# 128 rows of zeros behind both tables of edge sums, in a graph kernel on one core

## What is computed

```
dst = jnp.minimum((50000 * jax.random.uniform(..., (50000,)) ** 2.0).astype(jnp.int32), 49999)
_o = jnp.argsort(dst, stable=True)

# layer 0, added to x: attention over the incoming edges, gate, feed-forward
a = jnp.exp(alpha - m[dst])
denom = jax.ops.segment_sum(a, dst, num_segments=n) + 1e-16
a = a / denom[dst]
out = jax.ops.segment_sum(a[:, :, None] * v_j, dst, num_segments=n)
...
h2 = jax.nn.relu(h2 @ W1.T + b1) @ W2.T + b2

# layer 1, added to x: normalised sum over the incoming edges
x_i = x[from_]
x_j = x[to_]
m_j = norm[:, None] * (x_j + x_j * x_i @ W1_w.T + W1_b)
out = jax.ops.segment_sum(m_j, to_, num_segments=n)
```

## Time and profile before

| | us |
|---|---|
| timed executions: lowest, median, highest | 3546.07, 3553.65, 3562.57 |
| the profiled execution | 3554.38 |
| its span (first to last instruction) | 3552.5 |
| phase C, from the first fetch to the last | 3011.0 to 3533.4 |

### The profile page before, as it was taken

One profiled execution on the slowest core, in us unless ns is written; L12 is line 12 of the kernel. 1 busy time (PEld: TensorE's weight loads), 2 busy tenths in 40 slices (PEclk: granted clock), 3 DMA queues, 4 the chain that ended last, 5 costly groups with the idle time before them and its releaser, 6 DMA issues. The chain is left out here.

```text
span 3552.5 us, 56630 instructions
## 1 busy us (share of the span) xinstructions
PE 2248.5 (63%) x13730; PEld 1803.6 (51%) x13730; DVE 2280.3 (64%) x9173; ACT 1722.7 (48%) x4075; POOL 2301.1 (65%) x2429
## 2 busy tenths in 40 slices
PE   0002777777777773799999999997443442455554
PEld 0002667766667762566666666665333332444444
DVE  8886666666666664677877787775111111678778
ACT  8994333333333331678887888886111111344343
POOL 5554777777777771555555555551777775777776
PEclk9998999999999995899999999999555555555555
DMA  6553233333333332233333333341566664456676
GB/s 204 177 176 94 82 101 92 91 101 91 91 101 91 91 101 62 65 105 107 107 100 102 108 104 102 101 109 67 124 129 130 132 131 113 118 149 152 144 147 133
DMA packets 253888, 401.93 MB, mean 113 GB/s; under 512 B 56515, under 2 KB 165456, under 8 KB 253728
## 3 DMA queue, kind: packets, MB, share of 16 engines
q1 hardware_dynamic: 183670, 265.77, 25.2%
q0 software_dynamic: 63424, 133.57, 18.6%
q10 hardware_dynamic: 6682, 1.46, 0.2%
HBM read 241.74 MB, written 160.29 MB: 113 GB/s over the span
## 5 line engine op out<-in xcount | busy, mean ns | idle before, releaser
L1159 POOL DMA_INDIRECT agg<-rows,at_n x392 | 388.8, 992 | 144.4 <-issue 111.1
L1651 POOL DMA_INDIRECT aggc<-rows,at_nc x392 | 398.8, 1017 | 113.2 <-issue 104.8
L628 POOL DMA_INDIRECT zs<-z_table,at_s x392 | 381.0, 972 | 112.9 <-issue 104.7
L628 POOL DMA_INDIRECT zd<-z_table,at_d x392 | 375.0, 957 | 119.4 <-issue 105.7
L1476 POOL DMA_INDIRECT h2s<-h_table,at_s x392 | 372.8, 951 | 113.2 <-issue 90.9
L1224 PE MATMUL p_f<-z_t,w_t 128*128 128x512 f32 x784 | 377.4, 612 | 64.1 <-ACT act L1294 64.0
L1529 PE MATMUL p_sum<-h2s,same 128*128 128x129 f32 x784 | 208.1, 438 | 307.8 <-DMA h2s<-h_table,at_s 244.4
L1235 PE MATMUL p_f<-w_t,act 128*128 128x128 f32 x3136 | 383.8, 278 | 0.0
L1235 PEld LDWEIGHTS p_f<-w_t,act 128*128 128x128 f32 x3136 | 361.2, 192 | 22.2 <-issue 22.2
L1529 PEld LDWEIGHTS p_sum<-h2s,same 128*128 128x128 f32 x784 | 173.3, 318 | 342.5 <-issue 264.8
L1516 DVE TENSOR_SCALAR same<-dst_sb,dst_g 128x128 f32<-128x128 uint16 x392 | 84.0, 303 | 400.8 <-DMA dst_sb<-dst 392.5
(11 more groups left out here) (317 smaller groups left out, 6471.9 us busy)
## 6 DMA issues: line engine op xcount, KB each, us to landing
rows<-rows_sb SPq DMA_DIRECT2D x49, 576.0 KB
h_table<-h2b SPq DMA_DIRECT2D x49, 516.0 KB, 2.9
rows<-rows_sb SPq DMA_DIRECT2D x49, 516.0 KB
xa<-in_x_dram SPq DMA_DIRECT2D x49, 512.0 KB, 3.8
z_table<-za SPq DMA_DIRECT2D x49, 512.0 KB, 2.9
dst_sb<-dst SPq DMA_DIRECT2D x98, 256.0 KB
xb<-in_x_dram SPq DMA_DIRECT2D x49, 512.0 KB, 4.0
x_table<-x1b SPq DMA_DIRECT2D x49, 512.0 KB, 4.7
```

What stands on the lines that cost most here:

```text
L628: pool.indirect_dma_start(out=to[:, slot, k], out_offset=None, in_=z_table, in_offset=bass.IndirectOffsetOnAxis(ap=at[:, slot, k:k + 1], a ...
L1159: pool.indirect_dma_start(out=agg[:, ring, k], out_offset=None, in_=rows0, in_offset=bass.IndirectOffsetOnAxis(ap=at_n[:, ring, k:k + 1], ...
L1651: pool.indirect_dma_start(out=agg[:, slot, k], out_offset=None, in_=rows1, in_offset=bass.IndirectOffsetOnAxis(ap=at_n[:, slot, k:k + 1], ...
```

## The change

Behind the rows of the edges, both tables get 128 rows of zeros instead of one. The zeros in SBUF from which they are written grow from one partition to 128. POOL makes a column `none_at` with EP + p in partition p, by one more IOTA and one more copy. The middle takes this column in place of the number EP, so that a node without an edge fetches row EP + (its number modulo 128). The loops of B and C are untouched, and so is the zero row of `z_table`.

```
-    rows0 = dram("rows0", [EP + 1, ROW0])
-    rows1 = dram("rows1", [EP + 1, ROW1])
+    rows0 = dram("rows0", [EP + P, ROW0])
+    rows1 = dram("rows1", [EP + P, ROW1])
...
+        none_at = sb("none_at", [P, 1])
...
-            zrow = t("zrow", [1, ROW0])
+            zrow = t("zrow", [P, ROW0])
+            none_i = t("none_i", [P, 1], I32)
...
-                    act.dma_start(rows0[EP:EP + 1, :], zrow[:]).then_inc(padded, 16)
-                    act.dma_start(rows1[EP:EP + 1, :], zrow[:, 0:ROW1]).then_inc(padded, 16)
+                    act.dma_start(rows0[EP:EP + P, :], zrow[:]).then_inc(padded, 16)
+                    act.dma_start(rows1[EP:EP + P, :], zrow[:, 0:ROW1]).then_inc(padded, 16)
...
+                    chain.mark(g.iota(none_i[:], pattern=[[1, 1]], base=EP, channel_multiplier=1))
...
+                    g.tensor_copy(none_at[:], none_i[:]).then_inc(consts_set, 1)
...
-                    dve.wait_ge(consts_set, 2)
+                    dve.wait_ge(consts_set, 3)
...
-                    chain.mark(v.tensor_scalar(none[:], deg[:], 0.5, float(EP), ALU.is_lt, ALU.mult))
+                    chain.mark(v.tensor_scalar(none[:], deg[:], 0.5, none_at[:], ALU.is_lt, ALU.mult))
```

More of the change, by code:

```diff
@@ L408, in _ @@
                     act.dma_start(src_pad[E:EP].rearrange("(a b) -> a b", a=16), pad_z[:, 0:n].bitcast(I32)).then_inc(padded, 16)
-                    act.dma_start(z_table[N:N + 1, :], zrow[:, 0:D]).then_inc(padded, 16)
-                    act.dma_start(rows0[EP:EP + 1, :], zrow[:]).then_inc(padded, 16)
-                    act.dma_start(rows1[EP:EP + 1, :], zrow[:, 0:ROW1]).then_inc(padded, 16)
+                    act.dma_start(z_table[N:N + 1, :], zrow[0:1, 0:D]).then_inc(padded, 16)
+                    act.dma_start(rows0[EP:EP + P, :], zrow[:]).then_inc(padded, 16)
+                    act.dma_start(rows1[EP:EP + P, :], zrow[:, 0:ROW1]).then_inc(padded, 16)
                     nodes_a_scalar(act)
```

## The result

The changed kernel takes 3572.64 us (median of 7 executions, 3565.9 to 3575.66), the kernel before 3556.51 (7, 3546.07 to 3562.57). The ratio is 1.0043, with a 95% interval of 1.0029 to 1.0058: slower by about 15 us by the ratio, 16 by the medians. The forecast was 3569. The profiled execution took 3573.41 us, 3571.7 of them its span, against 3552.5 before: 19.2 us more. In the changed kernel the lines of B and C stand four higher (`aggc` L1655, `mixed` L1724, the two `basec` L1725 and L1727, `x1c` L1630, `leaky` L1736).

The account below looks back on a forecast made before the run. PE covers phase B's fetches and POOL paces phase C's; 26 groups by +0.79 and 13 by -0.38 us give +15.6, so 3554.4 + 15.6 = 3570.0, less 0.7 for the timed runs: 3569 us, range 3538 to 3584.

Parts of the forecast that it names:

- The zero rows and the column: At the start: larger zero writes, one IOTA, one CAST and the column operand cost 0, at most about 1 us once.
- Fetches in B land sooner: Phase B: fetches land up to 0.5 us sooner each, but PE covers them, so 0.
- Landings of C fall below the edge: Phase C: groups then alternate between late and early landings, +0.79 us each, +30.8 us if it holds through groups 9 to 47.
- L: Phase C: delay from the end of a group's last POOL call to DVE's `mixed`; expected 1.6 to 1.85 us.
- the edge: Phase C: delay between 1.61 and 1.87 us, last call to `mixed`; just above it a group hardly stalls, below it stalls.
- The price of the alternation: Phase C, groups 9 to 47: 26 alternating by +0.79 us and 13 at their best by -0.38, together +15.6 us.
- the alternation: Phase C: late and early landings in turn, SP's `x1c` load ahead of POOL's last call; 11.37 us a group.
- Just above the edge: Faster rival, phase C: landings settle where groups hardly stall, -14.8 us, 3540, or 3531 without the early spell; chance 0.20.
- Landings don't move: Rival: something other than the shared address slows late fetches, or the change is hidden; 3554 us, 3547 to 3562; chance 0.25.
- Nearly throughout: Slower rival, phase C: late and early landings alternate in 29 or more of 39 groups, up to 3585 us; chance 0.27.
- The rule of the Trainium skill on reads that start off a 256 byte boundary: Fetches: such reads take extra beats or transactions, so zero rows would get dearer and no landing sooner; spoke against the change.
- the saw: Phase C: POOL's stall against the delay from last call to `mixed`, repeating every 1.25 us, the distance of two calls.

Follow-up runs that it names:

- e1: Changed kernel, but all nodes without an edge fetch one address, the first of the 128 zero rows: 3554.77 us, 0.9993 of the kernel before.
- e2: Changed kernel with spread zero rows in phase B only, one address in phase C: 3554.84 us, 0.9994 of the kernel before.
- e4: Changed kernel with two small pause steps on DVE ahead of `mixed` in phase C: 3539.23 us, 0.995 of the kernel before.
- e9: Changed kernel using eight zero rows, one per fetch: 4124.87 us, 1.0041, on another chip where the kernel before took 4111.64 us.
- e10: Changed kernel using 16 zero rows, each 8 apart, the same in every fetch: 4124.35 us, 1.0029, on a chip where the kernel before took 4111.64 us.
- e11: Changed kernel, first `basec` of phase C made from one SBUF input, without bias: 4096.55 us, 0.998, on a chip where the kernel before took 4111.64 us.
- e8: Changed kernel with SP's load of `x1c` in phase C held until POOL has made the group's last call: 3548.52 us, 0.9957 of the kernel before.
- e6: Changed kernel with twelve pause steps on DVE ahead of `mixed` in phase C: 3544.3 us, 0.9951 of the kernel before.
- e5: Changed kernel with six pause steps on DVE ahead of `mixed` in phase C: 3564.65 us, 1.001 of the kernel before.

## Why the prediction was right, step by step

- **The zero rows and the column: 0.** Confirmed by e1 (0.9993).
- **Fetches in B land sooner, worth 0.** Confirmed: 2.5 us in place of 3.1, B of the same length with the same two waits, and e2 (0.9994). The forecast had said 2.6 to 2.8.
- **Landings of C fall below the edge.** Confirmed. L of the prompt groups is 1.62 to 1.84, and the edge lies between 1.71 and 1.83, as the copy goes; the prediction had it between 1.61 and 1.87 and took 1.6 to 1.85 for L. So the landings straddle the edge, and a good stretch never lasts.
- **The price of the alternation.** Here two terms were off, against each other. The prediction took two thirds of the groups 9 to 47 as alternating at 11.37 us and one third at their best, 26 by +0.79 and 13 by -0.38, +15.6. Measured: 34 of 39 are outside the good stretches, at (429.64 - 50.89)/34 = 11.14 each, where 50.89 is what groups 26 to 28 and 41 to 42 take together. So 34 by +0.56 and 5 by -0.40 came out, +17.0. The extent was too small and the price too high. That the forecast lay within 4 us of the time is luck in this part: the measured extent at the price taken would have been 34 by 0.79 less 5 by 0.38, +25, and the extent taken at the measured price 26 by 0.56 less 13 by 0.40, +9. The alternation is cheaper than in groups 2 to 8 because a late landing there is often only 3.6 to 4.1 us behind. DVE has then caught up by the next group (L = 1.77 in the rows above), and the calls behind it cost 1.0 us more than in a group at its best (11.10 us for group 14); after one of 4.5 us it has not (L = 2.61), and they cost 1.9 more (12.02 for group 4). A pair takes 21.8 us in the first case (groups 14 and 15) and 22.5 in the second (groups 4 and 5).
- **Not in the sum:** the last group, +2.0, which ended in the bad state, and 1.05 ahead of group 2. The latter is also just over the 1 us that the prediction allowed the phases before C; by the starts of C in e1 and e2 (3011.61 and 3008.53, with the same phases ahead of it) it is within what varies from one to another.
- **The rivals.** "Just above the edge" fell, though e4 shows that its price was right: with L at 1.85 to 2.1 in most groups the kernel takes 3539, where the rival said 3540. "Landings don't move" fell: they move, and by e1, e9 and e10 the shared address is the cause. "Nearly throughout" (3573 and more) was close: by extent it is what happened, by time it is the forecast's upper end.
- **The rule of the Trainium skill on reads that start off a 256 byte boundary** (DMA: Bandwidth & Descriptors, How a descriptor splits into AXI transactions), by which no landing would come sooner, did not decide. Of the changed kernel's rows of zeros for B, 576 bytes apart, three in four start off such a boundary if the table starts on one (that it does is assumed), and a packet takes 0.153 us against 0.218 with the single aligned row. In e10 all 16 are aligned, at 0.147, against 0.153 in e11 on the same chip, where three in four are not; for these rows the rule is worth no more than this difference.

**What holds POOL.** The prediction knew the saw, not its law. Laid side by side, the 392 calls and DVE's rows in the changed kernel give it. 28 calls that start 0.07 to 0.96 us into `mixed`, and 14 that start 0.04 to 0.07 us into the first `basec`, are held until 1.10 us after its start (its record is 1.23 us long). Nine of the first kind, after a group with L = 2.6 to 2.76, are held over the next instruction as well, 1.69 to 1.96 us in all. The 47 calls that start 0.05 to 0.61 us into `total`, which reads PSUM and SBUF, are not held. The short instructions of `out_sb`, which read `leaky` and `x1c`, lengthen calls too, most of them by 0.2 us or less. A call that is there first is not held either, and DVE's instruction then takes 1.27 us in place of 1.22 [e8's row at 3142.38].

The Trainium skill (SBUF — State Buffer, Who interferes with whom) says that GpSimd and VectorE take one pair of ports in turns, whoever issues first for its whole instruction, and the traces agree, but for the 0.13 us at the end: the hold ends 1.10 us into a row of 1.23. It also infers that a `tensor_tensor` does not hold up the writing of descriptors, and here every call that started well within one was held, by up to 1.0 us from a single one. The measurement decides; whether the call collides in reading its row numbers or in writing descriptors is not shown.

## What to carry to other kernels

A transfer that lands sooner moves whatever waits for it, and on an engine pair that blocks each other that alone can cost more than the transfer was worth. Before making a transfer cheaper, look at which calls start just before and just after the instructions that it releases; if their lengths jump between two values, the phase is what to set, for example with a short pause or a wait that fixes the order of a load. And padding that many lanes fetch should be spread over rows that differ within one fetch: here sixteen were enough.

## What the runs showed of the hardware that I had not expected

- Work of 0.25 us added to DVE made the kernel 0.5% faster (e4), and 1.5 us did the same (e6), while 0.7 us made it no faster than before (e5).
- An order that differs by 0.05 us (0.02 against 0.07 us behind `basec`) is worth 1.02 us to POOL.
- Many reads of one address within a fetch raise the mean time of a packet from 0.15 to 0.22 us; sixteen fixed rows do as well as 128, of which each fetch reads sixteen, and eight rows of which each fetch reads one do no better than one (0.23 us).
